# Second-layer attention weights converted in other rounds and parts, in a macaron transformer kernel on one core

## What is computed

```
x = x + 0.5 * FFN(LN(x))
x = x + GATT(LN(x))
x = x + 0.5 * FFN(LN(x))        # the same weights as the first time
```

## Time and profile before

| | us |
|---|---|
| median of 3 runs | 3641.99 |
| lowest, highest | 3641.96, 3644.24 |
| the profiled execution | 3643.0 |
| its span | 3641.3 |

### The profile page before, as it was taken

The page is one execution under the profiler, slowest core; times in us unless marked ns, Lnnn a source line. Parts: engine busy times, 40 slices in busy tenths (PEclk is TensorE's granted clock), DMA queues, the critical chain, the costliest instruction groups (busy, mean ns, idle before and its releaser), DMA issues.

```text
span 3641.3 us, 69393 instructions
## 1 busy us (share of the span) xinstructions
PE 3425.9 (94%) x20896; PEld 2802.7 (77%) x20896; DVE 2603.7 (72%) x7110; ACT 2077.7 (57%) x4852; POOL 2263.8 (62%) x2307
## 2 busy tenths in 40 slices
PE   4899998999999699999999999998999989999997
PEld 3678787777877588888888888886778877777775
DVE  6777887788888365665655656566788888888884
ACT  2576775677677244444444444444677667667664
POOL 3567676667766255555555555574667766777772
PEclk9899999999999899999999999998999999999999
DMA  4444443435445331212212122203444344434433
GB/s 149 143 150 140 133 158 122 141 130 163 146 131 175 88 73 44 47 47 54 59 44 45 50 51 59 71 30 113 140 133 158 124 133 164 146 124 153 162 118 116
DMA packets 429110, 403.04 MB, mean 111 GB/s; under 512 B 139832, under 2 KB 374296, under 8 KB 428728
## 3 DMA queue, kind: packets, MB, share of 16 engines
q1 hardware_dynamic: 428728, 398.49, 35.4%
HBM read 224.67 MB, written 159.38 MB: 105 GB/s over the span
## 4 chain that ended last, share of the span: by engine, by line
PE 76%; DVE 6%; issue 5%; DMA 4%; ACT 3%; POOL 3%; SPq 3%; POOLq 0%; DVEq 0%; ACTq 0%
PE psum L1497 21%; PE psum L1498 19%; PE psum L1499 19%; PE psum L1633 5%; PE psum L1616 4%; PE psum L1725 3%; PE psum L1605 2%; DMA pT<-p_turned 2%; ACT probs L962 2%; POOL ge_lo L859 1%; DVE probs L1203 1%; SPq L597 1%; POOL probs L820 1%; DMA w_hi<-w_lo 1%; POOL hid_lo L832 1%
## 5 line engine op out<-in xcount | busy, mean ns | idle before, releaser
L859 POOL TENSOR_TENSOR ge_lo<-ge,ge_hi 128x512 fp32r<-128x512 f32 x512 | 673.4, 1318 | 526.5 <-PE psum L1499 285.8
L820 POOL TENSOR_SCALAR probs<-probs,rz 128x256 f32<-128x256 f32 (+1 forms) x1024 | 449.4, 459 | 435.2 <-DVE rz L1217 434.6
L1035 ACT ACTIVATE ge<-psum 128x512 f32<-128x512 f32 x512 | 306.9, 600 | 669.2 <-PE psum L1725 666.8
L1394 DVE CAST ge_hi<-ge 128x512 fp32r<-128x512 f32 x512 | 265.1, 521 | 507.0 <-ACT ge L1035 504.7
L962 ACT ACTIVATE probs<-probs,nb,rq 128x256 f32<-128x256 f32 (+1 forms) x1024 | 577.3, 573 | 31.4 <-DVE nb L1211 29.9
L795 POOL TENSOR_TENSOR rinv<-ssq,minus_half 128x16 f32<-128x16 f32 x124 | 368.0, 2976 | 47.3 <-DVE ssq L1187 47.2
L1203 DVE CUSTOM_DVE_ANT_0 probs<-psum,mask 128x256 f32<-128x256 f32 (+1 forms) x1024 | 338.7, 386 | 60.6 <-PE psum L1616 46.5
L1497 PE MATMUL psum<-wqkv_hi,hT_hi 128*128 128x512 f32 x768 | 329.5, 429 | 13.9 <-DVE hT_lo L1161 7.3
L1225 DVE STREAM_TRANSPOSE p_blocks<-probs 128x384 f32<-128x384 f32 (+1 forms) x384 | 292.1, 786 | 46.1 <-POOL probs L820 22.8
L1498 PE MATMUL psum<-wqkv_hi,hT_lo 128*128 128x512 f32 x768 | 309.8, 403 | 0.0
L1499 PE MATMUL psum<-wqkv_lo,hT_hi 128*128 128x512 f32 x768 | 308.4, 402 | 0.0
(11 more groups left out here) (153 smaller groups left out, 9697.3 us busy)
## 6 DMA issues: line engine op xcount, KB each, us to landing
p_turned<-p_blocks SPq DMA_DIRECT2D x128, 512.0 KB, 2.9
pT<-p_turned SPq DMA_DIRECT2D x512, 128.0 KB, 2.8
p_turned<-p_blocks SPq DMA_DIRECT2D x128, 384.0 KB, 2.9
pT<-p_turned SPq DMA_DIRECT2D x512, 96.0 KB, 2.4
xnext<-stream SPq DMA_DIRECT2D x32, 512.0 KB, 3.8
xmid<-stream SPq DMA_DIRECT2D x32, 512.0 KB, 3.8
gaT<-y_turned SPq DMA_DIRECT2D x256, 64.0 KB, 2.0
y_turned<-probs SPq DMA_DIRECT2D x192, 64.0 KB, 2.9
```

The costliest lines, as they stand in the source:

```text
L820: last = nc.gpsimd.tensor_scalar(pu, pu, rz[:, h, t:t + 1], 1.0, ALU.mult, ALU.mult)
L859: nc.gpsimd.tensor_tensor(ges[1][:, k % 4, :], ge[:, k % 4, :], f32(ges[0][:, k % 4, :]), ALU.subtract).then_inc(S["g_lo"], 1)
L1035: nc.scalar.activation(ge[:, k % 4, :], RB[k % 2], ACT.Exp, scale=GSCALE, accum_out=gz[:, h, t:t + 1]).then_inc(S["g_exp"], 1)
```

## The change

- The conversion of wqkv is split in three parts instead of two, each 512 wide: keys (part 0), queries (1), values (2). Keys' conversions count on semaphores of their own (`wk_hi`, `wk_lo`).
- Keys' and queries' conversions for the next stage go from the head of round 7 to the tail of round 6, by new tokens `ik` and `iq` and a new argument `soon`; values' go from `i1` to a token `iv` late in round 7; the rope tables go from `i1` to a token `ir` at VectorE's head of round 7. VectorE now waits for `rope_ok` at the first `rq` of the new layer.
- On ScalarE and VectorE `i2` goes behind E7 and V7, `f0` and `f1` further back. `i0` and `i1` are gone. The lists of TensorE, GpSimd and SP stay.
- TensorE waits for values' conversion in round 8, at its first `v` product, for queries' and keys' in round 7 as before.

```diff
-ACT_STEPS = ("i0 +zh0 Kc2 Kc3 +zh1 -nh0 E0 -nh1 E1 i1 +sq0 E2 -G0 -G1 -u0 +sk0 -u1 -G2 E3 i2 E4 -G3 E5 -u2 -u3 "
-             "E6 -G4 O0 +sq1 +sk1 -G5 f0 E7 +sq2 -u4 -u5 f1 +sk2 O1 +Qc0 +sk3 O2 +Kc0 O3 +sq3 f2 +Kc1 +vh0 +vh1 "
-             "+Qc1 +vh2 +Qc2 +vh3 +Qc3").split()
-DVE_STEPS = ("X0 i0 -j0 -j1 +zl0 +zl1 X1 R0 -nl0 -nl1 X2 R1 V0 X3 V1 -y0 R2 -y1 i1 +rq0 +rk0 -y2 V2 X4 i2 R3 X5 "
-             "R4 V3 -y3 X6 +ss0 V4 R5 X7 V5 P0 +rq1 R6 +rk1 +ss1 -y4 R7 V6 -y5 f0 V7 +ss2 P1 -F f1 -e +rk2 +rq2 "
-             "P2 P3 +ss3 B x +rk3 +Y l +rq3 r f2").split()
+ACT_STEPS = ("+zh0 Kc2 Kc3 +zh1 -nh0 E0 -nh1 E1 +sq0 E2 -G0 -G1 -u0 +sk0 -u1 -G2 E3 E4 -G3 E5 -u2 -u3 E6 -G4 O0 "
+             "+sq1 +sk1 -G5 E7 i2 +sq2 -u4 -u5 f0 +sk2 iv O1 +Qc0 f1 +sk3 O2 +Kc0 ik O3 +sq3 iq f2 +Kc1 +vh0 "
+             "+vh1 +Qc1 +vh2 +Qc2 +vh3 +Qc3").split()
+DVE_STEPS = ("X0 -j0 -j1 ir +zl0 +zl1 X1 R0 -nl0 -nl1 X2 R1 V0 X3 V1 -y0 R2 -y1 +rq0 +rk0 -y2 V2 X4 R3 X5 R4 V3 "
+             "-y3 X6 +ss0 V4 R5 X7 V5 P0 +rq1 R6 +rk1 +ss1 -y4 R7 V6 -y5 V7 i2 +ss2 P1 f0 iv -F -e +rk2 +rq2 ik "
+             "f1 P2 P3 +ss3 iq B x +rk3 +Y l +rq3 r f2").split()
...
         for j in range(B - 4):
-            a_round(n0 + 3 + j)
+            a_round(n0 + 3 + j, soon=2 * call + 1 if j == B - 5 else None)
...
-    QKV_PARTS = (slice(0, 2 * INNER), slice(2 * INNER, 3 * INNER))
+    QKV_PARTS = [slice(i * INNER, (i + 1) * INNER) for i in (1, 0, 2)]
...
         def w_qkv(stage, part):
             k = w_base(stage)
-            for name in (("pe_q", "pe_k"), ("pe_v",))[part]:
-                need(act, S[name], NT * B * stage)
+            need(act, S[("pe_k", "pe_q", "pe_v")[part]], NT * B * stage)
             for kt in range(KD):
                 chunk_in(act, k + kt)
-            split_hi(k + part, [(wqkv_s[0][:, kt, QKV_PARTS[part]], w_buf(k + kt)[:, QKV_PARTS[part]], None) for kt in range(KD)])
+                last = copy(wqkv_s[0][:, kt, QKV_PARTS[part]], w_buf(k + kt)[:, QKV_PARTS[part]])
+            last.then_inc(S[("wk_hi", "w_hi", "w_hi")[part]], 1)
...
+                    if w == 0 and i == 0 and switch is not None and m == n + 1:
+                        dve.wait_ge(S["rope_ok"], switch + 1)
...
+                if kind == "ir" and switch is not None:
+                    w_rope(switch)
+                if kind == "ik" and soon is not None:
+                    w_qkv(soon, 0)
+                if kind == "iq" and soon is not None:
+                    w_qkv(soon, 1)
+                if kind == "iv" and switch is not None:
+                    w_qkv(switch, 2)
                 if kind == "i":
-                    if i == 1 and switch is not None:
-                        w_rope(switch)
-                    if i < KD and switch is not None:
-                        w_qkv(switch, i)
...
+                    if fresh_qkv is not None and w < 2 and m == n + 1:
+                        weights_done(pe, w_base(fresh_qkv) + 1)
+                        fresh_qkv = None
+                    if w == 2 and fresh_v is not None and m == n:
+                        weights_done(pe, w_base(fresh_v) + KD)
+                        fresh_v = None
```

More of the change, by code:

```diff
@@ L646, in first, with a_round @@
                 w_vectors(0)
-            def a_round(n, prev=True, nxt=True, load=None, switch=None, final=0, layer=0, call=call, early=None, after=None):
+            def a_round(n, prev=True, nxt=True, load=None, switch=None, final=0, layer=0, call=call, early=None, after=None, soon=None):
                 if call == 0 and not nxt:
@@ L920, in start, with some_steps @@
             weights_done(act, w_base(stage) + W_A)
-        for kt in range(KD):
-            w_qkv(0, kt)
+        for part in range(3):
+            w_qkv(0, part)
         w_o(0)
         stage_end(act, 0)
-        def some_steps(n, prev, nxt, only=None, load=None, switch=None, layer=0, table=ACT_STEPS, part=slice(None),
+        def some_steps(n, prev, nxt, only=None, load=None, switch=None, soon=None, layer=0, table=ACT_STEPS, part=slice(None),
                        home=bank):
@@ L1010, in first, with a_round @@
                 some_steps(n - 1, False, True, 1)
-            def a_round(n, prev=True, nxt=True, load=None, switch=None, final=0, layer=0, call=call, early=None, after=None):
-                some_steps(n, prev, nxt, None, load, switch, layer,
+            def a_round(n, prev=True, nxt=True, load=None, switch=None, final=0, layer=0, call=call, early=None, after=None, soon=None):
+                some_steps(n, prev, nxt, None, load, switch, soon, layer,
                            prepared(left(ACT_STEPS, BEGUN_ACT, load), PREP_ACT, call, nxt))
@@ L1049, in sequence @@
                         if which == "last" and k in W_NEXT:
-                            w_qkv(2, W_NEXT.index(k))
+                            for part in ((0, 1), (2,))[W_NEXT.index(k)]:
+                                w_qkv(2, part)
                         if which == "last" and k in AHEAD_ACT:
@@ L1103, in w_qkv @@
             k, cols = w_base(stage), QKV_PARTS[part]
-            split_lo(k + part, [(wqkv_s[1][:, kt, cols], wqkv_s[0][:, kt, cols], w_buf(k + kt)[:, cols], None) for kt in range(KD)])
-            if part == 1:
+            if part:
+                dve.wait_ge(S["w_hi"], k + part)
+            else:
+                dve.wait_ge(S["wk_hi"], stage + 1)
+            for kt in range(KD):
+                last = V.tensor_tensor(wqkv_s[1][:, kt, cols], w_buf(k + kt)[:, cols], f32(wqkv_s[0][:, kt, cols]), ALU.subtract)
+            last.then_inc(S[("wk_lo", "w_lo", "w_lo")[part]], 1)
+            if part == 2 and stage % LAYERS == 0:
                 dve.wait_ge(S["rope_ok"], stage + 1)
@@ L1150, in _, with some_steps @@
         w_rope(0)
-        for kt in range(KD):
-            w_qkv(0, kt)
+        for part in range(3):
+            w_qkv(0, part)
         w_o(0)
         stage_end(dve, 0)
-        def some_steps(n, prev, nxt, only=None, load=None, switch=None, final=0, layer=0, part=slice(None),
+        def some_steps(n, prev, nxt, only=None, load=None, switch=None, soon=None, final=0, layer=0, part=slice(None),
                        table=DVE_STEPS, home=bank):
@@ L1365, in first, with a_round @@
                 some_steps(n - 1, False, True, 1)
-            def a_round(n, prev=True, nxt=True, load=None, switch=None, final=0, layer=0, call=call, early=None, after=None):
-                some_steps(n, prev, nxt, None, load, switch, final, layer,
+            def a_round(n, prev=True, nxt=True, load=None, switch=None, final=0, layer=0, call=call, early=None, after=None, soon=None):
+                some_steps(n, prev, nxt, None, load, switch, soon, final, layer,
                            table=prepared(left(DVE_STEPS, BEGUN_DVE, load), PREP_DVE, call, nxt))
```

6 lines of the change are left out of this document (2 added, 4 removed).

## The result

| | median, us | runs | lowest to highest |
|---|---|---|---|
| before | 3642.04 | 5 | 3641.96 to 3645.53 |
| changed | 3624.30 | 5 | 3621.86 to 3627.45 |

The ratio to the kernel before is 0.9948, 95% interval 0.9935 to 0.9961: 17.7 us less, faster and outside the 0.2% that a measurement can tell. 3620.8 had been forecast, 3610 to 3631 as the range. The changed kernel's profiled execution took 3625.8 (span 3624.1), 1.5 above its median, against 3643.0 (span 3641.3) before: 17.2 less.

The account below looks back on a forecast made before the run. TensorE, 76% of the chain, was taken as the bound, through its gaps and clock. The switch's -22.0 and round 8's +0.8 sum to -21.2: 3621.8 us profiled, 3620.8 for the median, range 3610 to 3631.

Parts of the forecast that it names:

- rival (c): Contention at `ik` and `iv` and the longer head cost 7 instead of 3 a switch: 3628.8 us; chance 0.13.
- Round 7, what goes: Gaps of 4.38 and 5.06 us and both half-clock stretches go: -13.9 and -14.1 us in the two calls.
- Round 6, tail: `ik` ahead of P2 takes 2.5 us on VectorE; P2 ends at 552.9, W2 waits, and TensorE loses 0.9 us.
- Round 7, head: `ir` takes 1.5 us with GpSimd idle; TensorE loses 1.15 us at q0 and 0.35 at S3.
- rival (d): Round 7's head still waits for scale vectors, landing 2 us late, with half clock: +4.3 a call, 3629.4 us; chance 0.05.
- Round 8: Old gaps and half clock go, -10.2 us; a new 7.5 us gap before A5 and 3.1 of clock come: +0.4 a round.
- (a): Round 8 gains after all, `ld5` landing quickly or A5 not meeting SP's wait: 3615, or 3599.6 without gap; chance 0.14.
- (e): In round 8 A6 and A7 wait too, each with half clock; a round pays 26.5 us: 3652.6; chance 0.04.
- Rounds 0: In rounds 0 `wf2` waits for nothing new, and A5 and A7 wait for their loads as now: 0.
- All else: Beyond the rounds named, the last global sequence gets +0.3 us beside a TensorE that is the bound: counted 0.
- The rule and the row: `iq`'s second subtraction beside GpSimd's power operation: the trace row says no wait; the skill's exclusion rule says 2.3 us, 3625.4.
- Rival (b): GpSimd's power operation shuts VectorE out during `iq`'s second subtraction: +2.3 us a call, 3625.4; chance 0.08.

Follow-up runs that it names:

- the early scales: The changed kernel with P2 ahead of `ik` and `f1`, `wf2` behind ld7, and the two scale vectors loaded in round 1: 3602.7 us, ratio 0.9891.

## Why the prediction was right, and by how much it missed

By round lengths, changed minus before, call 0 and call 1, against the prediction's terms for both calls:

| step | predicted | measured |
|---|---|---|
| round 7, conversions gone, less its new head and `iv` | -28.0 + 4.2 = -23.8 | -11.6, -12.4 |
| round 6, tail (`ik` ahead of P2) | +1.8 | +3.8, +3.8 |
| round 8 | +0.8 | -1.9, -0.2 |
| rounds 0 | 0 | -2.9, +0.4 |
| all else | 0 | +3.8 together, of it 2.8 behind the last z |
| sum | -21.2 | -17.2 |

The range held, and the mechanism of rounds 7 and 8 held. That the sum came within 4 us is in part luck: the two rounds 6 cost 5.8 us more than forecast and the rest of the kernel 3.8, while rounds 8 and 0 gave 2.9 and 2.5 that had not been forecast. The switch as a whole (rounds 6 and 7) cost 6.1 and 5.5 us a call over two plain rounds where 3.0 had been put. That is nearer to the 7 of rival (c), though not by its mechanism: no gap reached 3 us, and contention at `ik` was not the cause: in the run with P2 first it took 2.39 us beside an addition, and round 6 was a plain 66.74.

**Round 7, what goes:** right. Both gaps went, and the two runs that put one part each back brought its gap and half clock back (4.4 to 4.9 and 5.4 to 6.1 a round). That adds up to 9.8 to 11.0 of the 11.6 to 12.4 that the round lost. Where the rest belongs was not tried.

**Round 6, tail: the step that failed** is "Then P2 ends at 552.9 where W2 started at 551.95: TensorE loses 0.9". The cost of `ik` was right (2.4 for 2.5), and P2 ended 0.2 us from where it had been put. But the first on TensorE to need P2 is not W2: it is q3, 1.5 us earlier (550.45 in the plain round), which writes the bank that P2 reads. The gap was 2.18 instead of 0.9, and with it came 3.3 us at half clock, which the sum did not have: 3.8 instead of 0.9 a call. Putting P2 first took all of it away.

**Round 7, head:** right in size. `ir` took 1.5 us with GpSimd idle, and TensorE stood 1.5 and 0.9 us behind zl0, where 1.15 + 0.35 had been put; in call 0, 0.48 us of this is VectorE's wait for the scale vector, rival (d) in small. The waiter was again another than forecast, and again because of a bank: not q0 but n1 just ahead of it, which writes the bank that zl0 reads. With `iv`, rounds 7 took 2.3 and 1.7 us over the plain 66.75, for 2.1 forecast. `iv` took 2.68 on VectorE beside GpSimd and cost TensorE 0.34 (0.6 had been put).

**Round 8:** right. The gap was 7.12 and 7.11 (7.5), its releaser a transfer, its place A5, `wf2` behind V7 and `i2`; the half clock behind it granted 6.2 us of work at 0.50 in call 0. In call 1 only 6.8 us of half clock were granted, about half of them inside the gap. Rivals (a) and (e) are out: the wait was there, and A6 and A7 did not wait. The 1.5 us before q3 in call 1 is the same bank again, behind `f1`; the prediction had that covered by A5's delay, which it is not.

**Rounds 0:** 0 had been put. The gap before A5 in call 0 was 1.8 for 3.5 and half clock 3.3 us shorter; in call 1 it was 2.1 for 1.8. Call 1 also had a wait of 1.5 us for a transfer at a second A group, which the kernel before did not have. Which of this belongs to the change and which to the execution stays open: the gap before A5 was 0.7 to 3.8 us in the other runs that left `wf2` in place.

**All else:** mostly the stretch behind the last z, 172.3 us for 169.5, with a mean granted clock of 0.95 for 0.96. No instruction of it was changed. The other profiles lie at 169.2 to 169.4 or at 171.2 to 173.0, so this is taken for an execution's own, which the forecast could not have had.

**The rule and the row.** VectorE's `iq` subtractions, started at 554.80, took 1.31 us beside a power operation that ran from 554.97 for 3.28: no wait for VectorE, as the row of before had said, and against what the Trainium skill, "SBUF — State Buffer", section "SBUF: two separate sides", would have had. In all eight kernels with `iq` in the tail, and in both calls, the second subtraction started inside the power operation and took 0.70 to 0.71 us. Rival (b) is out. GpSimd paid 0.4 (3.28 for 2.91). Beside GpSimd's shorter operations VectorE did wait: `ik` took 2.36 us beside additions for the 1.31 of `iq`, and the rope operations in the middle of round 7 lost 1.1 to 1.4 us at a time. There the rule and the runs agree in kind.

## What to carry to other kernels

When work is put ahead of an operation in a full schedule, look for its first waiter through every resource that it frees, the accumulator's bank too, and not only through its result: here the bank was wanted 1.5 us earlier than the result. A conversion that frees a buffer also releases the load that is issued into it, and whatever stands behind that load in the same queue: move the load with it. An edit that measures as nothing on one kernel, as `wf2`'s did here, can be worth 17 us once another wait is gone.

## What was not expected of the hardware

- A gap of 2.18 us before q3 was followed by 3.4 us of half clock in every profile that had it but one (call 1 of the run with `i2` back: 69.0 us for 70.6). Gaps of 2.0 to 2.5 us at the head of round 7 were followed by one in two cases of four, gaps of 0.9 to 1.8 there never. But the 1.74 us gap in round 8 of call 1, in the kernel before with `wf2` moved, had one behind it, which the same gap in call 0 and in both calls of the kernel before had not. So gaps of one size went either way here, and the runs do not say what decides it.
- The scale vector, 32 KB, landed 5.3 us after its issue behind two transfers of 512 KB, and 5.9 in the run with P2 first; its landing and not the 512 KB table's released VectorE.
- With the same instructions in them, rounds 0 differ by up to 2.3 us between profiled executions and the last stretch by up to 3.8, through half-clock stretches and waits for transfers. That is as large as the terms that a change of this size is argued from, and is why what the early scales are worth in all can be read round by round but not in the median.
